# A routed mixture-of-experts row with six gates, six destinations and six expert indices in place of 64 gates and 64 ranks

## The reference

```
router_logits = x @ router_w.T + bias                       # 64 experts
router_probs  = softmax(router_logits)
topk_p, topk_i = top_k(router_probs, 6)
topk_p = topk_p / (sum(topk_p) + 1e-9)                      # six gates
...
expert_in[e, slot] = x_flat[token]                          # tokens sorted by expert, capacity C
expert_out = (silu(expert_in @ w_gate.T) * (expert_in @ w_up.T)) @ w_down.T
sparse[token] += gate * expert_out                          # six experts for each token
return shared_out + sparse
```

## Time and profile before

| | |
|---|---|
| median of 3 runs | 3905.64 us (3903.35 to 3913.82) |
| the profiled execution: its time | 3897.31 us |
| its span, first to last instruction | 3895.1 us |
| POOL busy | 2732.0 us, 70% |
| PE busy / PEld busy | 2718.1 us, 70% / 2046.7 us, 53% |
| DVE busy | 2392.7 us, 61% |
| ACT busy | 1624.1 us, 42% |
| mean granted TensorE clock | 0.698 |

### The profile page before, as it was taken

How to read it: one execution, slowest core, us unless ns; L and a number is a source line. 1 busy time by engine, 2 the same in 40 slices (tenths; PEclk the granted TensorE clock), 3 DMA queues, 4 the chain that set the end, 5 groups by cost and what they waited for, 6 DMA issues and landing times. The chain is left out here.

```text
span 3895.1 us, 72768 instructions
## 1 busy us (share of the span) xinstructions
PE 2718.1 (70%) x13864; PEld 2046.7 (53%) x13865; DVE 2392.7 (61%) x8787; ACT 1624.1 (42%) x4042; POOL 2732.0 (70%) x4427
## 2 busy tenths in 40 slices
PE   5888888647767777777676635777777777777660
PEld 4666666523443443444343325666667666666660
DVE  6788888746666667676666733444444444466754
ACT  4666666633434343333334312343434334333330
POOL 3555555302888788878768888888888888888881
PEclk9888888855565555555556656788877777777775
DMA  6555555231333333333223345444444444589858
GB/s 262 186 191 196 190 194 194 89 89 59 118 118 118 110 117 116 113 97 107 88 84 96 92 141 153 140 142 138 139 141 142 138 134 139 159 278 287 252 162 269
DMA packets 448700, 582.01 MB, mean 149 GB/s; under 512 B 64858, under 2 KB 388858, under 8 KB 437076
## 3 DMA queue, kind: packets, MB, share of 16 engines
q1 hardware_dynamic: 364356, 411.44, 35.2%
q0 software_dynamic: 83232, 162.29, 12.3%
q10 hardware_dynamic: 944, 6.67, 0.6%
HBM read 299.55 MB, written 306.56 MB: 156 GB/s over the span
## 5 line engine op out<-in xcount | busy, mean ns | idle before, releaser
L1020 POOL DMA_INDIRECT xed<-xr,idxs x1014 | 1006.4, 992 | 420.5 <-POOL pace L1025 178.2
L1032 POOL DMA_INDIRECT ytk<-yo,idxy x1080 | 1082.3, 1002 | 246.7 <-POOL pace L1037 208.4
L1258 PE MATMUL wide<-wdt,hT 64*128 x2160 | 374.4, 323 | 411.0 <-DVE hT L1748 410.2
L1413 ACT ACTIVATE yo<-wide,gd 128x128 f32<-128x128 f32 x1080 | 307.8, 368 | 685.0 <-PE wide L1258 642.9
L1730 DVE TENSOR_TENSOR idxy<-xin 128x1 int32<-128x1 f32 x1080 | 147.9, 162 | 708.3 <-DMA ytk<-yo,idxy 707.2
L1258 PEld LDWEIGHTS wide<-wdt,hT 64*128 64x128 f32 x2160 | 315.9, 222 | 468.3 <-issue 466.9
L1240 PE MATMUL bank<-wgu,xeT 128*128 x2160 | 393.6, 343 | 0.0
L1240 PEld LDWEIGHTS bank<-wgu,xeT 128*128 128x128 f32 x2160 | 372.6, 259 | 2.1 <-issue 0.8
L557 POOL TENSOR_TENSOR big<-big,scb 128x1024 f32<-128x1024 f32 (+1 forms) x43 | 125.2, 2911 | 336.9 <-ACT big L674 329.5
L1174 PE MATMUL wide<-xn,e 128*128 128x128 f32 (+3 forms) x1024 | 293.3, 414 | 0.0
L546 POOL TENSOR_TENSOR weff<-w,gam 128x640 f32<-128x640 f32 x169 | 261.0, 1573 | 41.0 <-DMA scb<-in_scales 31.6
(11 more groups left out here) (309 smaller groups left out, 5614.4 us busy)
## 6 DMA issues: line engine op xcount, KB each, us to landing
xin<-xed SPq DMA_DIRECT2D x1080, 113.0 KB
ytk<-zeros SPq DMA_DIRECT2D x42, 1536.0 KB, 9.7
yg<-ytk SPq DMA_DIRECT2D x42, 1536.0 KB
xs<-in_xcol SPq DMA_DIRECT2D x42, 1280.0 KB, 6.8
ytk<-yo,idxy POOLq DMA_INDIRECT x1080
xed<-xr,idxs POOLq DMA_INDIRECT x1014
H<-in_ximg SPq DMA_DIRECT2D x4, 2704.0 KB, 18.2
h1d<-H SPq DMA_DIRECT2D x42, 256.0 KB, 2.0
```

The source lines that it names most:

```text
L1020: p.indirect_dma_start(xed[:, :], bass.IndirectOffsetOnAxis(ap=idxs[:, slot, j, k:k + 1], axis=0), xr[:, slot, j, :], None, bounds_check=Z ...
L1032: p.indirect_dma_start(ytk[:, :], bass.IndirectOffsetOnAxis(ap=idxy[:, slot, j:j + 1], axis=0), yo[:, slot, j, :], None, bounds_check=128 ...
L1258: last = pe.matmul(eO[slot % 2][:, j * D:(j + 1) * D], hT[:, slot % 2, j, :], wdt[:, bass.ds(e, 1), :].rearrange("p o f -> p (o f)"), star ...
L1413: last = a.activation(yo[:, slot, j, :], eO[slot % 2][:, j * D:(j + 1) * D], ACT.Copy, scale=gd[:, slot, j:j + 1])
```

## The change

The row shrinks from 226 to 148 floats (592 bytes): 128 for the token, 8 indices (of the eight largest, so the six experts stand in places 2 to 7), 6 gates, 6 destinations. The six gates are six exponentials of the six largest logits, not 64 masked ones; the indices come from `max_index`. In the expert stage DVE no longer reads registers: it compares the six indices of each row with the block's expert, multiplies gates and destinations by the match, and sums over six. For this the table of experts is wanted in all 128 partitions, as floats (`texpb`). The offset `OUTSIDE` (2^20) is taken off the stored destinations and put back after the sum, so that rows without a match go nowhere. SP's `load_rows` waits for `found_r` (the product) in place of `idxy_r`. Cut to its core:

```diff
+XI = D
+XG = XI + 8
+XD = XG + TOPK
+XW = XD + TOPK
...
@@ POOL, start of back and scatter
-            p.memset(zrow[:, 0:XB], 0.0)
-            p.memset(zrow[:, XB:XW], OUTSIDE).then_inc(n["s_c"], 1)
+            p.memset(zrow[:, :], 0.0).then_inc(n["s_c"], 1)
+            p.iota(jki[:, :], [[1, TG * TOPK]], base=-int(OUTSIDE), channel_multiplier=0)
...
-                p.wait_ge(n["rank_r"], g + 1)
-                p.wait_ge(n["base_r"], g + 1)
+                p.wait_ge(n["goal_r"], g + 1)
...
@@ SP, load_rows
-                after(sp, n["idxy_r"], q - ES + 1)
+                after(sp, n["found_r"], q - ES + 1)
...
@@ PE, lists_early (and rA in lists_late alike)
-                        last = pe.matmul((rA, rC)[i][0:1, 0:m], ones[0:NE + 1, 0:1], src[:, w:w + m],
+                        last = pe.matmul((rA, rC)[i][:, 0:m], ones[0:NE + 1, :], src[:, w:w + m],
...
@@ ACT, probs and copy_y
+                a.wait_ge(n["d6_r"], g + 1)
+                after(a, n["row_r"], g)
+                a.activation(e6[:, 0:tiles_of(g), :], d6[:, 0:tiles_of(g), :], ACT.Exp).then_inc(n["e6_r"], 1)
...
-                a.wait_ge(n["gd_r"], q + 1)
+                a.wait_ge(n["gi_r"], q + 1)
...
-                                        scale=gd[:, slot, j:j + 1])
+                                        scale=gi[:, slot, j, 0:1])
...
@@ DVE, choose: between match_replace and mask
+                v.wait_ge(n["nl_r"], g + 1)
+                after(v, n["e6_r"], g)
+                v.tensor_tensor(d6[:, 0:nj, :], t8[:, 0:nj, 2:8],
+                                top1[:, slot % 2, 0:nj].unsqueeze(2).to_broadcast([128, nj, TOPK]), ALU.add).then_inc(n["d6_r"], 1)
...
@@ DVE, denominator
-                v.tensor_tensor(lr[:, 0:nj, 0:NE], ex[:, 0:nj, :], mask[:, 0:nj, :], ALU.mult).then_inc(n["em_r"], 1)
-                v.wait_ge(n["em_r"], g + 1)
-                v.tensor_reduce(s6[:, 0:nj], lr[:, 0:nj, 0:NE], AX.X, ALU.add).then_inc(n["s6_r"], 1)
+                v.nop(nofuse=True)
+                for j in range(nj):
+                    last = v.max_index(xri[:, slot, j, XI:XI + 8], t8[:, j, :], lo[:, j, :])
+                last.then_inc(n["which_r"], 1)
+                v.wait_ge(n["e6_r"], g + 1)
+                v.tensor_reduce(s6[:, 0:nj], e6[:, 0:nj, :], AX.X, ALU.add).then_inc(n["s6_r"], 1)
...
-                for j in range(nj):
-                    last = v.tensor_tensor_scan(xrk[:, slot, j, 2 * XK:2 * XB], onesb[:, 0:NE], mask[:, j, :],
-                                                float(TOPK * j - 1), ALU.mult, ALU.add)
-                last.then_inc(n["rank_r"], 1)
-                v.tensor_scalar(xr[:, slot, 0:nj, XB:XW], token[:, 0:1].unsqueeze(1).to_broadcast([128, nj, 2]), 0.0, None,
-                                ALU.add).then_inc(n["base_r"], 1)
-                v.wait_ge(n["base_r"], g + 1)
+                v.tensor_scalar(xr[:, slot, 0:nj, XD:XW], jk[:, 0:nj, :], token[:, 0:1], None, ALU.add).then_inc(n["goal_r"], 1)
+                v.wait_ge(n["goal_r"], g + 1)
...
-                v.scalar_tensor_tensor(xr[:, slot, 0:nj, XG:XK], lr[:, 0:nj, 0:NE], 0.5,
-                                       rden[:, 0:nj].unsqueeze(2).to_broadcast([128, nj, NE]), ALU.mult, ALU.mult)\
+                v.scalar_tensor_tensor(xr[:, slot, 0:nj, XG:XD], e6[:, 0:nj, :], 0.5,
+                                       rden[:, 0:nj].unsqueeze(2).to_broadcast([128, nj, TOPK]), ALU.mult, ALU.mult)\
...
@@ DVE, before the stages, tables_early, tables_late
+            link(v.tensor_copy(jk[:, :, :].rearrange("p j k -> p (j k)"), jki[:, :]))
...
+                        if dst is texp:
+                            link(v.tensor_copy(texpb[:, w:w + m], (rA, rC)[i][:, 0:m]))
                         link(v.tensor_copy(dst[:, w:w + m], (rA, rC)[i][0:1, 0:m]))
...
+                link(v.tensor_copy(texpb[:, M0:NT], rA[:, 0:m]))
...
@@ DVE, pick
-                experts = entries(DVE, texp, TG * q, TG, NE - 1)
                 v.wait_ge(xin_in[slot], 64 * (rnd + 1))
+                after(v, n["found_r"], q)
+                v.tensor_tensor(match[:, :, :], xini[:, slot, :, XI + 2:XG],
+                                texpb[:, bass.ds(TG * q, TG)].unsqueeze(2).to_broadcast([128, TG, TOPK]), ALU.is_equal)\
+                    .then_inc(n["match_r"], 1)
+                v.wait_ge(n["match_r"], q + 1)
+                after(v, n["gi_r"], q)
+                v.tensor_tensor(found[:, :, :, :], xin[:, slot, :, XG:XW].rearrange("p j (a k) -> p j a k", a=2),
+                                match[:, :, :].unsqueeze(2).to_broadcast([128, TG, 2, TOPK]), ALU.mult).then_inc(n["found_r"], 1)
+                v.wait_ge(n["found_r"], q + 1)
                 after(v, n["yo_r"], q - ES + 1)
-                v.nop(nofuse=True)
-                for j, e in enumerate(experts):
-                    last = v.tensor_copy(gd[:, slot, j:j + 1], xin[:, slot, j, bass.ds(e + XG, 1)])
-                last.then_inc(n["gd_r"], 1)
+                v.tensor_reduce(gi[:, slot, :, :], found[:, :, :, :], AX.X, ALU.add).then_inc(n["gi_r"], 1)
+                v.wait_ge(n["gi_r"], q + 1)
                 if not isinstance(q, int) or q >= ES:
                     v.wait_ge(yo_out[slot], 16 * TG * rnd)
-                for j, e in enumerate(experts):
-                    last = v.tensor_tensor(idxy[:, slot, j:j + 1], xink[:, slot, j, bass.ds(e + 2 * XK, 1)],
-                                           xin[:, slot, j, XB:XB + 1], ALU.add)
-                last.then_inc(n["idxy_r"], 1)
+                v.tensor_scalar(idxy[:, slot, :], gi[:, slot, :, 1], OUTSIDE, None, ALU.add).then_inc(n["idxy_r"], 1)
```

More of the change, by code:

```diff
@@ L17 @@
 I32 = mybir.dt.int32
+U32 = mybir.dt.uint32
 RMAX = bass.bass_isa.ReduceOp.max
@@ L40 @@
 ZR = NE * CR
-XG = D
-XK = D + NE
-XB = D + NE + NE // 2
-XW = XB + 2
+XI = D
+XG = XI + 8
+XD = XG + TOPK
+XW = XD + TOPK
 NY = T * TOPK
@@ L881, in back @@
     xr = sb("xr", [128, 4, TG, XW])
-    xrk = xr[:, :, :, :].bitcast(BF16)
+    xri = xr[:, :, :, :].bitcast(U32)
     mask = sb("mask", [128, TG, NE], BF16)
@@ L897, in back @@
     ttail = sb("ttail", [1, NE], I32)
+    texpb = sb("texpb", [128, NT])
+    jki = sb("jki", [128, TG * TOPK], I32)
+    jk = sb("jk", [128, TG, TOPK])
     token = sb("token", [128, 1])
@@ L935, in back @@
     zz = sb_early("zz4", [128, TG])
+    d6 = sb_early("d6", [128, TG, TOPK])
+    e6 = sb_early("e6", [128, TG, TOPK])
     s6 = sb_early("s6", [128, TG])
@@ L944, in back @@
     xin = sb("xin", [128, ES, TG, XW])
-    xink = xin[:, :, :, :].bitcast(BF16)
+    xini = xin[:, :, :, :].bitcast(U32)
     xeT = sb("xeT", [128, 2, TG, 128])
@@ L951, in back @@
     yo = sb("yo", [128, ES, TG, D])
-    gd = sb("gd", [128, ES, TG])
+    match = sb("match", [128, TG, TOPK])
+    found = sb("found", [128, TG, 2, TOPK])
+    gi = sb("gi", [128, ES, TG, 2])
     idxy = sb("idxy", [128, ES, TG], I32)
@@ L962, in back @@
                  "rep_r", "mask_r", "nl_r", "cum_done", "slot_r", "valid_r", "dest0_r", "dest_r", "taken_r",
-                 "dk_r", "zk_r", "idx_r", "rank_r", "base_r", "token_r", "ex_r", "em_r", "s6_r", "den_r", "rden_r", "row_r",
+                 "dk_r", "zk_r", "idx_r", "which_r", "goal_r", "token_r", "ex_r", "d6_r", "e6_r", "s6_r", "den_r", "rden_r", "row_r",
                  "th_r", "sa_r", "hs_r", "sh_done", "h4_r",
                  "first_v", "first_p", "early_v", "early_p", "late_v", "late_p", "tab_ready", "tail_z", "paced",
-                 "xet_done", "xeT_r", "geu_done", "the_r", "ae_r", "hh_r", "ht_done", "hT_r", "dn_done", "gd_r", "idxy_r", "yo_r",
+                 "xet_done", "xeT_r", "geu_done", "the_r", "ae_r", "hh_r", "ht_done", "hT_r", "dn_done", "match_r", "found_r", "gi_r", "idxy_r", "yo_r",
                  "add1_r", "add2_r", "add3_r", "ot_r"):
@@ L994, in back @@
     eO = (wide[1][:, 0:512], wide[1][:, 512:1024])
-    SP, PE, DVE = mybir.EngineType.SP, mybir.EngineType.PE, mybir.EngineType.DVE
+    SP, PE = mybir.EngineType.SP, mybir.EngineType.PE
     with nc.Block() as block:
@@ L1293, in lists_late @@
                     pe.wait_ge(n["late_v"], 3 + part)
-                    pe.matmul(rA[0:1, 0:m], ones[0:NE + 1, 0:1], oh[:, 0:m], start=(part == 0), stop=(part == 2))
+                    pe.matmul(rA[:, 0:m], ones[0:NE + 1, :], oh[:, 0:m], start=(part == 0), stop=(part == 2))
                     pe.matmul(rC[0:1, 0:m], ones[0:NE + 1, 0:1], itin[:, 0:m], start=(part == 0), stop=(part == 2))\
```

## The result

| | before | changed |
|---|---|---|
| median | 3901.47 us (6 runs, 3890.69 to 3913.82) | 3928.26 us (6 runs, 3921.45 to 3941.07) |
| ratio, 95% interval | | 1.0078 [1.0056, 1.0099] |
| profiled execution, span | 3895.1 us | 3919.5 us |
| mean granted TensorE clock | 0.698 | 0.683 |

The changed kernel is slower by 27 us, outside the range of the prediction (3874 to 3917) and on the other side of no change. First the table by stage of the changed kernel (columns as in the earlier trace rows; the last row is the tail, from the last spread on).

The account below looks back on a forecast made before the run. PE, DVE and ACT were taken to pace routing, POOL to bound the kernel from the spreads on. Routing +3.9 and woven part -14 us gave -10 us: 3905.6 - 10.1 = 3895.5 us, range 3874 to 3917.

Parts of the forecast that it names:

- Routing, +3.9 us: Routing stage: 3.5 + 1.0 + 0.2 - 0.85 us, later at the last row that POOL waits for.
- the 0.85 us saved: Row's end in routing: 1.8 us in place of 2.6 a group, covered by DVE's wait for shared_down, counted once.
- `d6`: Extra 24-element DVE operation ahead of mask in routing: 0.1 us a group, 35 groups, +3.5 us (0 to 7.4).
- `texpb`: Copies of the expert table in DVE's early chain while POOL runs dry: +1.0 us, up to 1.5 with semaphores.
- second rival: Routing: DVE's time is the bound, so 35 groups each keep 0.85 us; 3866 us in all, chance 0.10.
- Quiet stage, 0: Expert stage before the sums are woven in: DVE's shorter work is covered and POOL waits for nothing, 0 us.
- third rival: Expert stage: new small two-input DVE operations stop POOL, 0.15 us x 270 = 40 us; 3936 us, chance 0.10.
- Woven part, -14 us: Spreads from about 3385 us, with sums woven in: a shorter path to `yo` cuts POOL's waits, -14 us (0 to -20).
- third piece: Woven part: loads of rows wait for `found`, finished before the landing wait; worth nothing by itself.
- First rival: Woven part: the sum's 1536 KB still delay the landing, so the shorter path only lengthens DVE's wait; 3909.5 us, chance 0.22.
- Tail, 0: Last 84 us, 13 sums bound by transfers that the change doesn't touch: 0 us.
- Another clock: Routing: PE's granted clock shifts, a pair changes by 1 us, 17 us in all; 3878 or 3912 and above, chance 0.08.

Follow-up runs that it names:

- late release: The changed kernel with one line undone: load_rows waits for idxy_r, behind the landing, again. 3884.53 us, 0.9976 of the kernel before, where that took 3898.53 us.
- early release alone: The kernel before, old rows and gates, with the loads of rows released ahead of the landing wait: 3944.86 us, 1.0137 of the kernel before, where that took 3898.53 us.
- job 5: Fifth batch of follow-up runs, with the kernel before rerun unchanged: 3898.53 us; the changed kernel took 1.0084 of it.
- The run made to isolate that: The changed kernel, rows still released early, but SyncE holds the sum's transfer until idxy_r: 1.0014 of the kernel before, beside 1.0019 for the changed kernel.
- job 3: Third batch of follow-up runs: the kernel before took 4904.61 us and the changed kernel 1.0019 of it.
- theories A and C: Explanations of the loss: A, early release sends the sum's transfer ahead of awaited scatters; C, DVE's shorter work after the landing locks a four-quad cycle.

## Why the prediction was wrong, step by step

**Routing, +3.9 us: the larger pieces were right, the sum can't be seen.** The four `max_index` and the row's end in the changed kernel, DVE in order of time, against the earlier trace rows:

```profile
1268.34 0.08 DVE L1596 MATCH_VALUE_LOAD xr<-t,lo 128x8 f32 x1
1268.41 0.22 DVE L1596 FIND_INDEX8 xr<-t,lo 128x8 uint32<-128x66 f32 x1
...
1269.13 0.16 DVE L1599 TENSOR_REDUCE s<-e 128x4 f32<-128x24 f32 x1
...
1269.93 0.17 DVE L1609 SCALAR_TENSOR_TENSOR xr<-e,rden 128x24 f32<-128x24 f32 x1
```

The four take 0.79 us (0.88 taken from `match_replace`), all of it 1.76 us in place of 2.6: the 0.85 us saved are there. And they are covered as argued. The wait behind them, to be set against the earlier trace rows:

```profile
DVE h L1619 <- PE wide L1230: 122.8, 36, 4.5
```

That is 3.4 us each, where it was 2.6, as the forecast said. `d6` costs little: from the start of the last `MATCH_REPLACE8` to that of the operation behind `mask`, 0.46 us before and

```profile
1285.19 0.20 DVE L1539 MATCH_REPLACE8 lr<-t,lo 128x66 f32<-128x66 f32 x1
1285.32 0.16 DVE L1543 TENSOR_TENSOR d<-t,top 128x24 f32<-128x24 f32 x1
1285.43 0.29 DVE L1546 TENSOR_SCALAR mask<-lr 128x256 bf16<-128x256 f32 x1
1285.64 0.68 DVE L1552 SCALAR_TENSOR_TENSOR sa<-th,wide 128x512 f32<-128x512 f32 x1
```

0.45 us here. Over all 43 groups the median of this distance is 0.46 us in each of the six traces, with `d6` and without, and the means are 0.49 to 0.52 in both. So `d6` cost nothing that can be seen, the lower end of the 0 to 0.21 us a group that the prediction bounded, and its 3.5 us were too much. `texpb` took 1.0 us for its two early copies (0.69 and 0.31), as forecast. But the first spread, which the term was to shift, starts at 2360.6, 2365.0 and 2351.6 in the three traces with the old routing and at 2356.2, 2366.6 and 2359.7 in the three with the new: means of 2359.1 and 2360.8, in a scatter of 7 us either way. A term of 4 us is smaller than what this stage varies by from one execution to the next. The -4.4 us between the two traces above is that scatter and no sign of a gain. The second rival (the routing stage keeps 0.85 us a group, -29 us) has no support.

**Quiet stage, 0: right.** 725.1 us busy and 156.3 us idle, where it was 724.9 and 156.3.

**Collisions of the new small operations with POOL (third rival, the slower one): false.** `match` and `found` ran in each of the quads, and the 746 spreads kept their mean of 972 ns. "Slower" came true, but not by this rival's way. The long additions do disturb POOL as before: in the woven part the mean is 1058 to 1067 ns with the new picks, 1082 to 1100 with the old ones.

**Woven part, -14 us: the term that failed, by one of its three pieces.** The two pieces on DVE's path (one operation in place of four after the landing, smaller transfers of rows) were priced at -14 us with ends of 0 and -20. Measured with the release as it was, they are -18.1 us (1450.4 to 1432.3), inside these ends, and the kernel with them, 0.9976 of before, lies near the -10 us of the whole forecast (-9 us by the ratio, -14 by the medians). The signs that the prediction named are there too: idleness ahead of a woven spread of 68.3/288 = 0.24 us (forecast: from 0.28 towards 0.21) at a mean of 1067 ns. In the changed kernel that idleness is 0.42 us, past the 0.28 that was to show the forecast wrong. The third piece was dismissed in one sentence: loads wait for `found`, "since PE waits little for `xin`, that is worth nothing by itself". It looked only at who waits for the rows. It did not follow the moved release through SyncE's queue: behind the loads of rows stands the sum's transfer of 1536 KB, and it moved with them. The trace of before already held the parts: the transfer goes out at 3562.39 together with `add_up` at 3562.31, and so within 1.9 us for all 28. There DVE's own four microseconds of work run beside it; with the early release half of the transfers run while DVE waits. Measured in place of the 0: +50 us with the new picks, +45 with the old.

**First rival, the wait moves back to the sum's transfer (3909.5 us): right in its object, wrong in its size.** It named the transfer ahead of the landing, but took it as fixed and only able to eat the gain. With the release that the change gave it, it moved, and cost more than the gain.

**Tail, 0: right.** 81.3, 85.0 and 82.8 us with the change or its late release, 84.2 and 83.7 before (85.9 with the early release alone). **Another clock:** the changed kernel's woven part has 0.73 where it was 0.75, its quiet one 0.76 and, in job 5, 0.81, and POOL's spreads there are the same in both. It decides nothing here.

What is shown: the release is the cause of the loss, since undoing that line alone takes away the pauses and 47 us, and bringing it into the old kernel brings them and 46 us. What is read from the order in six traces, and not isolated by a run: that it acts through the sum's transfer. The run made to isolate that was inconclusive.

## What to carry to other kernels

When an edit lets a DMA issue wait for an earlier event, follow not the data but the queue: everything behind it on that engine moves too, and a large transfer two places behind can be the one that matters. A wait that looks useless may be what puts a long transfer beside work that needs no landing, as the orders above suggest; before it is made shorter, look up in the trace what goes out just behind it and what lands next. And compare effects with what a stage varies by from execution to execution: here three traces with the same routing code differ by up to 13 us at the end of that stage, while the 1080 spreads after it repeat to 0.2 us from one execution of a kernel to another.

## What was unexpected of the hardware

**A second condition of the chip, 24 to 26% slower, in four of five jobs.** The same kernel before took 3898.53 us in one job and 4841 to 4917 us in four. The record has chip 11 for job 3 and for job 5, with 4904.61 and 3898.53 us, so the number of the chip doesn't tell which condition it is in. In the trace of the changed kernel from job 3 (span 4902.8 us) everything up to about 940 us is as in the other traces; the extra pauses begin with POOL's first scatter. DVE is busy 682.1 us of the first 900, as in job 5 (681.3), but from 940 to 1300 us 150.7 in place of 234.8. These rows, in order of time, stand from 8 us behind it on:

```profile
947.86 1.12 PE L1189 MATMUL wide<-ident,xr 128*128 128x128 f32 x4
...
951.19 0.60 ACT L1384 ACTIVATE x4T<-wide 128x512 f32<-128x512 f32 x1 [10.65 <-remote]
...
951.84 1.97 PE L1200 MATMUL wide<-rwt,x4T 128*128 128x64 f32 x8 [2.87 <-issue]
...
963.35 0.42 DVE L1529 TENSOR_TENSOR lo<-wide,rbias 128x256 f32<-128x256 f32 x1 [16.16 <-issue]
```

ACT starts 2.2 us after PE has written what it copies (948.98), DVE 9.5 us after the end of the product that it reads (953.81); these operations, once they run, take about as long as elsewhere. In the expert stage there POOL loses its lead (2700 to 4200 us):

```profile
L1039 POOL DMA_INDIRECT ytk<-yo,idxy x724 | 705.5, 974 | 516.0 <-issue 468.8 <-ACT yo L1423 27.4 <-POOL pace L1044 19.8
```

The spread still takes 974 ns, but 0.71 us of idleness stand ahead of one where 0.21 is usual (156.3/746). What causes these pauses was not found. Their consequence for such a study was: under them the 50 us effect of the release was at most 0.25% in any job, and theories A and C could only be told apart when the chip was back at 3899 us. A ratio of two kernels holds for the condition in which it was taken.

**Additions in SBUF and POOL's transfers.** In the late release kernel a spread beside the wide addition took 2.38 us in place of 0.97:

```profile
3564.26 2.38 POOL L1039 DMA_INDIRECT ytk<-yo,idxy  x1
```

The addition ran from 3564.04. So it was in the kernel before (2.35 us). In both, the sum's transfer went out at the same moment as the addition, so that it could be at fault as well. The early release parts the two: in the changed kernel of job 5 seventeen spreads were issued within 1.5 us behind a sum's transfer with no addition running, and none took over 0.972 us, while those beside a large addition go up to 2.51 us. That leaves the addition; the Trainium skill (SBUF — State Buffer, "Who interferes with whom") infers the opposite for the writing of descriptors. The small two-input products `match` and `found` show no such effect (972 ns).
